# Plain fp32 products for the first mixing and for four of twelve convolution shifts, without a stagger

## The reference

```
def mixing(x, e, W0, b0, W1, b1, W2, b2, weight, bias_k):   # layers 0 and 2
    h = gelu(gelu(e @ W0 + b0) @ W1 + b1)
    att = softmax(h @ W2 + b2)                    # 8 experts
    agg_w = einsum('bk,koi->boi', att, weight)    # a 128x128 matrix for each sample
    return einsum('boi,bih->boh', agg_w, x) + (att @ bias_k)[:, :, None]

def conv(x, c, weight, c_weight, bias):           # layers 1 and 3: 9 taps, 4 groups of 32 channels
    out = conv1d(x, weight, padding=4, groups=4)
    return out + (c @ c_weight.T)[:, :, None] + bias[None, :, None]

x = x + mixing0(x); x = x + conv1(x); x = x + mixing2(x); x = x + conv3(x)
```

## Time and profile before

| | us |
|---|---|
| median of 3 runs | 2906.19 (2905.75 to 2907.77) |
| profiled execution, its own time | 2907.99 |
| its span | 2905.7 |
| TensorE busy | 2882.7 |
| VectorE busy | 2420.1 |
| ScalarE busy | 1668.6 |
| GpSimd busy | 1482.6 |
| DMA queue 1, share of 16 engines | 63.8% |

### The profile page before, as it was taken

The page is one execution under the profiler, slowest core; times in us unless marked ns, Lnnn a source line. Parts: engine busy times, 40 slices in busy tenths (PEclk is TensorE's granted clock), DMA queues, the critical chain, the costliest instruction groups (busy, mean ns, idle before and its releaser), DMA issues.

```text
span 2905.7 us, 122950 instructions
## 1 busy us (share of the span) xinstructions
PE 2882.7 (99%) x49240; PEld 2860.9 (98%) x49240; DVE 2420.1 (83%) x2589; ACT 1668.6 (57%) x2593; POOL 1482.6 (51%) x1546
## 2 busy tenths in 40 slices
PE   8999999999999999999999999999999999999998
PEld 7999999999999999999999999999999999999998
DVE  8888888888888888888888888888888888888884
ACT  5555555555555555556565656565556555655564
POOL 3445554555455545544554455445544554455452
PEclk9999999999999999999999999999999999999999
DMA  6777777777777777777777777777777777777774
GB/s 160 198 199 201 202 196 203 198 202 196 202 197 202 198 202 196 204 196 204 193 204 197 204 193 206 198 203 194 204 199 203 197 200 200 202 203 193 201 202 138
DMA packets 374536, 573.17 MB, mean 197 GB/s; under 512 B 63336, under 2 KB 226800, under 8 KB 358128
## 3 DMA queue, kind: packets, MB, share of 16 engines
q1 hardware_dynamic: 325744, 506.17, 63.8%
q10 hardware_dynamic: 48768, 66.65, 9.1%
HBM read 271.63 MB, written 167.77 MB: 151 GB/s over the span
## 4 chain that ended last, share of the span: by engine, by line
PE 98%; DVE 1%; ACT 0%; DMA 0%; issue 0%; ACTq 0%; SPq 0%
PE ps L354 74%; PE ps L339 24%; ACT x_t L530 0%; DVE prod L592 0%; DVE y L635 0%; DVE m_sum L595 0%; PE ps L267 0%; PE ps L262 0%; DMA mixed<-m_own 0%; DVE m_own L603 0%; DMA m_parts<-mixed 0%; DVE m_own L601 0%; DVE xp L627 0%; DVE conv_parts L567 0%; ACT L449 0%
## 5 line engine op out<-in xcount | busy, mean ns | idle before, releaser
L354 PE MATMUL ps<-y,conv_parts 32*128 32x512 f32 x36864 | 2735.2, 390 | 2.2 <-DVE y L635 2.2
L354 PEld LDWEIGHTS ps<-y,conv_parts 32*128 32x128 f32 x36864 | 2533.4, 184 | 17.5 <-issue 2.3
L500 ACT ACTIVATE y<-ps,bias 128x512 fp32r<-128x512 f32 x1536 | 1045.4, 690 | 748.6 <-PE ps L354 710.6
L635 DVE SCALAR_TENSOR_TENSOR y<-ps,bias,y 128x512 fp32r<-128x512 f32 x1536 | 1074.4, 747 | 417.4 <-ACT y L500 415.0
L703 POOL COPY bias<-bias_table 128x4 f32 (+3 forms) x512 | 99.1, 209 | 1383.3 <-DMA o_ch<-o_ph 1344.5
L709 POOL TENSOR_TENSOR xp<-x_t,xp 128x512 fp32r<-128x512 f32 x508 | 787.4, 1581 | 3.9 <-ACT xp L469 3.9
L339 PE MATMUL ps<-xp,m_parts 32*128 32x512 f32 x6144 | 653.2, 391 | 7.5 <-DVE y L635 3.7
L339 PE MATMUL ps<-y,m_parts 32*128 32x512 f32 x6144 | 652.4, 390 | 0.0
L716 POOL COPY o_t<-o_ch 128x512 f32<-128x512 f32 x508 | 630.1, 1358 | 8.4 <-DMA o_ch<-o_ph 8.4
L533 ACT ACTIVATE o_ph<-ps,bias 128x512 f32<-128x512 f32 x508 | 330.5, 686 | 435.6 <-PE ps L354 431.1
L339 PEld LDWEIGHTS ps<-xp,m_parts 32*128 32x128 f32 x6144 | 557.9, 184 | 10.3 <-issue 4.1
(11 more groups left out here) (53 smaller groups left out, 53.3 us busy)
## 6 DMA issues: line engine op xcount, KB each, us to landing
x_t<-x SPq DMA_DIRECT2D x512, 256.0 KB, 5.6
m_parts<-mixed SPq DMA_DIRECT2D x1020, 128.0 KB, 3.7
out<-o_t SPq DMA_DIRECT2D x127, 1024.0 KB, 4.0
o_ch<-o_ph SPq DMA_DIRECT2D x1016, 64.0 KB, 2.0
o_ch<-o_ph ACTq DMA_DIRECT2D x1016, 64.0 KB, 3.7
mixed<-m_own SPq DMA_DIRECT2D x256, 128.0 KB, 2.1
conv_raw<-conv_w SPq DMA_DIRECT2D x2, 768.0 KB, 11.8
mix_sb<-mix_w SPq DMA_DIRECT2D x2, 576.0 KB, 9.1
```

Source lines behind the costliest of these rows:

```text
L354: ins = nc.tensor.matmul(ps[:, 4 + t, :], conv_parts[layer][rows, w, PH * q + p_in, :], src[rows, a, p_in, q:q + N], start=(k == 0), stop= ...
L500: nc.scalar.activation(dst, src, ACT.Identity, bias=bias[layer][:, k % WIDTH[layer]:k % WIDTH[layer] + 1]).then_inc(high_set[layer], 1)
L635: nc.vector.scalar_tensor_tensor(out=dst, in0=src, scalar=bias[layer][:, k % WIDTH[layer]:k % WIDTH[layer] + 1], in1=high.bitcast(fp32), o ...
```

## The change

- **First mixing** works on whole x in plain fp32: four products of 128 rows by 128 columns by 512, with m_sum[0] as it comes from VectorE. x is no longer split, m_parts, the store and the load remain for the second mixing alone, and the spreading product for sample 0 is gone. x comes by one DMA in its own order.
- **Convolutions.** The shifts 2 to 9 (DENSE) stay in three f32r passes on four row tiles, 24 rounds. The shifts 0, 1, 10 and 11 have no weights for some output phases; they (SPARSE) are made in plain fp32 on tiles of 32 rows by 64 columns, 16 products a convolution in two sets of eight that lie on eight different tiles. They read a plain fp32 copy (y1_full, y3_full) that ScalarE makes with an additional evacuation of layers 0 and 2, and the unrounded conv_raw. Convolution 3 begins with them, convolution 1 ends with them.
- **LOW** of layers 0 and 2 is made from that copy in SBUF, so those banks are free when ScalarE is done (high_set).
- **No stagger**: the four tiles of a stage start and end together.
- **ScalarE issues no DMAs**; SyncE issues all of them, in a new order.
- **The tail**: the last sample's o_ph is regrouped by 16 small fp32 products (last_regroup) and copied to x_t in time order by ScalarE and VectorE, a quarter at a time.

```diff
+    DENSE = range(2, SHIFTS - 2)
+    SPARSE = (((1, 0, 2), (10, 2, 2)),
+              ((0, 0, 2), (11, 2, 2)))
 # SyncE
+                if has(i, inner, 0) and has(i, inner, -1):
+                    sp.wait_ge(mm[0], 4 * (i + 1))
+                    load_x(i + 1)
                 if has(i, inner, 3):
                     sp.wait_ge(in_time_set, 4 * (i - 2))
                     sp.dma_start(out[i - 3], o_t[:]).then_inc(out_done, 16)
+                if moves:
+                    for g in range(G // 2):
+                        shuffle(i - 2, g)
+                if has(i, inner, 0):
+                    store_matrix(i)
+                if moves:
+                    for g in range(G // 2, G):
+                        shuffle(i - 2, g)
+                if has(i, inner, 0):
+                    load_matrix(i, not inner and i == 0)
 # TensorE
+            def first_mix(i, inner):
+                pe.wait_ge(summed[0], i + 1)
+                pe.wait_ge(x_in, 16 * (i + 1))
...
+                for q in range(G):
+                    if inner or i >= 2:
+                        pe.wait_ge(high_set[2], nth(i - 2, q))
+                    nc.tensor.matmul(ps[:, q, :], m_sum[0][:], x_t[:, q, :], start=True, stop=True).then_inc(mm[0], 1)
+            def sparse(layer, src, begins, wait_bank):
+                for r, units in enumerate(SPARSE):
+                    for t in range(G):
+                        rows = slice(CG * t, CG * (t + 1))
+                        if r == 0 and begins:
+                            wait_bank(t)
+                        for s, p, width in units:
+                            q, p_in = divmod(s, PH)
+                            final = r == len(SPARSE) - 1 and not begins
+                            ins = nc.tensor.matmul(ps[CG * p:CG * (p + width), 4 + t, :],
+                                                   conv_raw[layer][rows, 128 * s + CG * p:128 * s + CG * (p + width)],
+                                                   src[rows, p_in, q:q + N], start=(r == 0 and begins), stop=final)
+                            if final:
+                                ins.then_inc(mm[1], 1)
+            def step(i, inner):
...
+                if now:
+                    first_mix(i, inner)
+                if not inner and i == 0:
+                    att_to_all(1)
+                if before:
+                    if not inner and i == 2:
+                        pe.wait_ge(conv_set, 2)
+                    pe.wait_ge(high_set[2], 4 * (i - 1))
+                    sparse(3, y3_full, True, free3)
+                    pe.wait_ge(low_set[2], 4 * (i - 1))
+                    dense(3, y3, False, free3)
+                if last:
+                    second_mix(i, inner)
+                if now:
+                    if not inner and i == 0:
+                        pe.wait_ge(zeros_set, 1)
+                        pe.wait_ge(conv_set, 1)
+                    pe.wait_ge(low_set[0], 4 * (i + 1))
+                    dense(1, y1, True, free1)
+                    if not inner and i == 0:
+                        side_bias()
+                        pe.wait_ge(full_first, G)
+                    sparse(1, y1_full, False, free1)
+            def last_regroup():
+                pe.wait_ge(phases_set, 4 * B)
+                for p in range(PH):
+                    for g in range(G):
+                        rows = slice(CG * p, CG * (p + 1))
+                        nc.tensor.matmul(ps[CG * g:CG * (g + 1), p, :], consts_sb[rows, CG * p:CG * (p + 1)], o_ph[rows, g, :],
+                                         start=True, stop=True).then_inc(regroup_mm, 1)
 # ScalarE
+            def high(layer, j, k, src, dst, full=None):
...
+                if full is not None:
+                    nc.scalar.activation(full, src, ACT.Identity, bias=column)
+                nc.scalar.activation(dst, src, ACT.Identity, bias=column).then_inc(high_set[layer], 1)
 # VectorE
+            def low(layer, j, k, dst, full, high):
+                dve.wait_ge(high_set[layer], nth(j, k))
+                nc.vector.tensor_tensor(dst, full, high.bitcast(fp32), ALU.subtract).then_inc(low_set[layer], 1)
             def step(i, inner):
...
+                elif now:
+                    if inner or i + 1 < B:
+                        matrix(0, i + 1)
+                    for q in range(G):
+                        low(0, i, q, segment(y1[:, LOW], q), segment(y1_full, q), segment(y1[:, HIGH], q))
+                    matrix(2, i)
+                    halves(i)
```

More of the change, by code:

```diff
@@ L128, in build_cond_resid @@
         x_in = sem("x_in")
[L129 removed]
+        m_in = sem("m_in")
         shuffled = [sem(f"shuffled{p}") for p in range(PH)]
@@ new lines, in dense @@
+            def dense(layer, src, begins, wait_bank):
+                order = sorted(DENSE, key=lambda s: (s % PH, s))
+                for k, s in enumerate(order):
+                    q, p_in = divmod(s, PH)
+                    for n, (w, a) in enumerate(PASSES):
+                        first = k == 0 and n == 0 and begins
+                        final = k == len(order) - 1 and n == len(PASSES) - 1 and not begins
+                        for t in range(G):
+                            rows = slice(CG * t, CG * (t + 1))
+                            if first:
+                                wait_bank(t)
+                            ins = nc.tensor.matmul(ps[:, 4 + t, :], conv_parts[layer][rows, w, s - DENSE[0], :],
+                                                   src[rows, a, p_in, q:q + N], start=first, stop=final)
+                            if final:
+                                ins.then_inc(mm[3], 1)
@@ L535, in step @@
-                if not inner and i == 0:
-                    conv_high_part(3)
+                        nc.scalar.activation(o_ph[:, g, :], ps[:, 4 + g, :], ACT.Identity,
+                                             bias=bias[3][:, g:g + 1]).then_inc(phases_set, 1)
+                    if final:
+                        act.wait_ge(regroup_mm, G * PH)
+                        act.wait_ge(mm[0], 4 * B)
+                        for q in range(G):
+                            dst, src = last_in_time(q, 0)
+                            nc.scalar.copy(dst, src).then_inc(last_set[q], 1)
@@ new lines, in step @@
+                    att_rows(5, 1, 1)
+                    matrix(2, 0, first=True)
+                    halves(0, first=True)
+                    dve.wait_ge(table_act, 2)
+                    dve.wait_ge(table_dve, 2)
+                    matrix(0, 1)
+                elif now:
+                    if inner or i + 1 < B:
+                        matrix(0, i + 1)
+                    for q in range(G):
+                        low(0, i, q, segment(y1[:, LOW], q), segment(y1_full, q), segment(y1[:, HIGH], q))
+                    matrix(2, i)
+                    halves(i)
@@ L681, in _ @@
             for beside in (y1, y3):
-                last = nc.gpsimd.memset(beside[:, :, :, 0:HALO:HALO - 1].bitcast(fp32), 0.0)
+                nc.gpsimd.memset(beside[:, :, :, 0:HALO:HALO - 1].bitcast(fp32), 0.0)
+            for beside in (y1_full, y3_full):
+                last = nc.gpsimd.memset(beside[:, :, 0:HALO:HALO - 1], 0.0)
             last.then_inc(zeros_set, 1)
```

398 lines of the change are left out of this document (130 added, 268 removed).

## The result

| | before | after |
|---|---|---|
| median, us | 2905.97 (4 runs) | 2831.89 (4 runs, 2830.63 to 2833.21) |
| span of the profiled execution | 2905.7 | 2830.7 |
| period of a sample in the steady part | 22.31 | 21.76 |
| all that is not 126 periods | 94.6 | 88.9 |

The ratio is 0.9744, 95% interval 0.9727 to 0.9761. The forecast was 2849 us with a period of 21.92 and 86.8 us for the rest.

What follows compares the result with a forecast made beforehand. TensorE was taken as the bound. Start and end of 86.8 us plus 126 x 21.92 gave a span of 2848.7 us; adding 2.3 and subtracting 1.8 gave 2849 us, range 2775 to 2965.

Steps and rivals of the forecast that it cites:

- The bound: Whole kernel: TensorE busy 2882.7 of 2905.7 us at granted clock 1.0 throughout, with a period of 22.31 us a sample.
- An fp32 record: TensorE, plain fp32: each product shows as two records, each 0.436 us for 512 columns, bounds 0.427 and 0.465.
- Eight tiles at once: Sparse phases: eight 64-column tiles run together, 1.74 us instead of 2.79, gaining 1.05 twice a sample.
- The rival of the column halves: Sparse phases: column halves of one row group take turns, 3.49 us instead of 1.74; 3296 us, chance 0.07.
- The second record: Sparse phases: a product's second record holds up the next tile, 7.41 us a phase; 4301 us, chance 0.08.
- Shape changes: TensorE: four changes of tile shape a sample, 0.70 us together, bounds 0 and 1.2.
- The faster rival: TensorE: shape changes hidden, 0.427 us a record, but the first stall grows to 0.36; 2776 us, chance 0.14.
- The first stall: First mixing to convolution 3: TensorE waits for banks to be emptied, 0.1 us a sample, bounds 0 and 0.4.
- The second stall: Second mixing to convolution 1: TensorE waits for ScalarE to free four banks, 0.2 us a sample, bounds 0 and 0.5.
- The sum: Per sample on TensorE: records 6.98, 60 rounds 13.94, shape changes 0.70, stalls 0.30, together 21.92 us against 22.31.
- The engines beside: Other engines: VectorE about 80% busy, ScalarE 75%, GpSimd near 27%; matrix and x loads priced at nothing.
- Start and end: Outside the 126 steady periods: 86.8 us instead of 94.6; step 1 begins at 31.0, step 2 at 49.3, end 37.5.

Runs made afterwards that it cites:

- e1: Kernel after with the fp32 shifts on 128-column tiles, four products at a time instead of eight: 3225.83 us, ratio 1.1100 to the kernel before.
- e2: Kernel after with the same 16 sparse products a phase queued tile by tile: 2866.44 us, ratio 0.9860 to the kernel before.
- e4: Kernel after with each convolution's f32r shifts and sparse rounds alternated in halves, adding four tile shape changes a sample: 2934.5 us, ratio 1.0099 to before.
- e5: Kernel after with first mixing as 12 f32r rounds on constant tiles, layer 0 not computed: 2829.14 us, ratio 0.9735 to the kernel before.
- e6: Kernel after with VectorE writing the fourth bank of o_ph, ScalarE the first three: 2818.27 us, ratio 0.9697 to the kernel before.
- e7: Kernel after with six shifts in fp32, adding two rounds of sixteen 32 by 32 tiles: 2837.38 us, ratio 0.9765 to the kernel before.
- e9: e7 with one more round of sixteen zero-weight 32 by 32 tiles in each convolution: 3107.99 us, ratio 1.0694 to the kernel before.
- e3: Kernel after with all twelve shifts back in three f32r passes: 3076.11 us, ratio 1.0582 to the kernel before.
- e8: Kernel after with the changes of e6 and e7 together: 2819.76 us, ratio 0.9706 to the kernel before.

## Why the prediction was right, point by point

**The bound.** As said, TensorE before and after, and the period carries the result: 126 x (22.31 - 21.76) = 69 us of the 75 by which the span fell. One reading was too smooth: the earlier trace rows show 90% or more in every slice, not 1.0 throughout. In the trace of before the granted clock is 0.5 from 36.1 to 39.5 us and from 56.6 to 60.0, and so the 94.6 us outside the steady part already held time at half clock.

**An fp32 record.** Put at 0.436 us within 0.427 and 0.465; the eight records of first mixing lie 0.429 us apart (the first gap, which holds part of the shape change, is 0.53), the low end, as the small fp32 products of the earlier trace rows had it. Sixteen of them are 0.11 us less than forecast.

**Eight tiles at once.** The step that decided the sign. It held: in the window from 1508.1 to 1508.25 of the kernel after, the first records of eight products are already at work,

```profile
1508.18 0.69 PE L343 MATMUL ps<-y_full,conv_raw 32*64 32x512 f32 x8
```

0.69 us for all eight where one alone is modelled at some 0.6, and e1 shows the price without it. The rival of the column halves would have given 3296 us; e1, which is that rival made by hand but has two shape changes fewer, gave 3226.

**The second record.** The rival by which one product's second record holds up the next tile is refuted, by the kernel after and more strongly by e2. So the rule of the Trainium skill, page TensorE: Matmul & The Clock Gate, section Part 3, that products start and end in strict order, does not hold for plain fp32 products on different tiles; the measurement decides. Giving it 0.08 was fair from a trace that had no such case, and what spoke against it was the right sign.

**Shape changes.** Put at 0.70 for four. In the stage table they are inside the intervals: 3.63 for first mixing is 8 x 0.429 = 3.43 and 0.20; 1.90 for a sparse phase is 4 x 0.429 = 1.72 and 0.18. The sum of four is 0.7 to 0.8, and e4 puts 0.20 on each. That the shape costs it and not the format is shown with e4, by e1. The faster rival, changes hidden behind the queue, is out.

**The first stall** (convolution 1 to first mixing to convolution 3) was put at 0.1. It is 0: convolution 3's sparse part starts 3.63 after first mixing, with no gap beyond the shape change. The term was mis-sized by 0.1, because the 0.2 us for registers in the loop does not come here: L477 starts 0.11 after L314 does, an estimated 0.19 after the end of the last sparse product's stream (its start at 1509.57 and 0.427), where 0.2 to 0.4 had been allowed. And TensorE goes on 0.07 after VectorE's last low half (1510.91 + 2.73 = 1513.64) where 0.1 to 0.26 had been allowed. What the prediction did not see is how close this balance is: e5 shows that here evacuation and first mixing are the same 3.6 us.

```profile
1510.19 2.42 ACT L477 ACTIVATE y<-ps,bias 128x512 fp32r<-128x512 f32 x4 [2.89 <-PE ps L343]
1510.91 2.73 DVE L609 SCALAR_TENSOR_TENSOR y<-ps,bias,y 128x512 fp32r<-128x512 f32 x4 [2.89 <-ACT y L477]
```

**The second stall** (o_ph) was put at 0.2; e6 takes away 0.15. Its place and its releaser were right.

**The sum.** 16 records 6.86, 60 rounds 13.94 to 14.0, changes 0.7 to 0.8, second stall 0.15: 21.7 to 21.8, measured 21.76. The forecast's 0.16 too much are the records (0.11) and the first stall (0.1), less some hundredths in the f32r rounds.

**The engines beside.** VectorE was put at 80% and is at 69%. The subtractions took 0.81 rather than 0.69 us, but the multiplication (L592 before, L573 after) fell from 2.09 to 1.64 and the two halves (L601 and L603, now L585 and L587) from 1.02 and 0.85 to 0.23 and 0.29:

```profile
L573 DVE TENSOR_TENSOR prod<-mix_sb,att_table 128x1152 f32<-128x1152 f32 x254 | 416.6, 1640 | 0.0
...
L587 DVE TENSOR_TENSOR m_own<-m_sum,m_own 128x128 fp32r<-128x128 f32 x128 | 37.4, 292 | 4.4
L585 DVE CAST m_own<-m_sum 128x128 fp32r<-128x128 f32 x128 | 29.1, 227 | 15.8
```

I had carried over means of operations that are long when GpSimd is at work beside them, although showed it. In the trace of before, the 27 of 256 L603 that no GpSimd instruction overlaps take 0.29 us each and the others 0.91 on average; in the kernel after none is overlapped, and all 128 take 0.29. No run varied GpSimd's work alone. GpSimd itself came to 31% for 27. ScalarE came to 65% for 75, as its evacuations overlap in part (0.577 apart at 0.7 each). In the steady part neither is on the path; ScalarE's 1% of the chain comes from the start and the end, where TensorE waited for it (7.8 us in all). The matrix and x came in time; no wait on a DMA is in the chain.

**Start and end.** Put at 86.8, measured 88.9. The end came to 36.9 against 37.5: the 5.4 us stall is there as 4.9, the regrouping took 1.15 for 1.5, the copies 2.0 to 2.5 for 3.8. But the stall brought what the prediction left out: TensorE stood still for 4.86 us and then ran at half clock for the sparse phase, 3.52 us from start to start instead of 1.90. The last line is from the view by stretches: stretch, length, TensorE busy and records, granted clock, DMA share, GB/s.

```profile
2812.67 3.59 PE L343 MATMUL ps<-y_full,conv_raw 32*64 32x512 f32 x32 [4.86 <-ACT y L477]
2816.19 5.86 PE L361 MATMUL ps<-y,conv_parts 32*128 32x512 f32 x96
...
2823.71 1.15 PE L415 MATMUL ps<-o_ph,consts_sb 32*32 32x512 f32 x32 [1.67 <-DVE o_ph L648]
...
2812.70:2816.00 3.30, 3.30 (x32) 0.50 0.40 98
```

The start is where the 2.1 us went: step 1 begins at 32.54, not 31.0, and step 2 at 52.04, not 49.3, 2.7 late against the 0.6 that the end gave back. Second mixing in step 1 waits one bank at a time as foreseen. In this execution the small products of line 261 ran at half clock:

```profile
11.20 3.21 PE L261 MATMUL ps<-consts_sb,att_sb 128*128 128x128 f32 x16
14.34 0.71 PE L291 MATMUL ps<-att_t,mix_b_sb 8*128 8x128 f32 x4
```

3.21 us where the earlier trace rows has 2.05, and first mixing begins at 15.63 instead of 13.5.

The rest of the delay is in step 1. Its second mixing waits bank by bank, the last time until 40.01, and then the granted clock is 0.50 from 41.0 to 44.4 us:

```profile
40.01 4.30 PE L329 MATMUL ps<-y,m_parts 32*128 32x512 f32 x44 [0.66 <-ACT y L477]
```

Convolution 1 starts 4.09 us after this start. In the trace of e4, where the clock stays at 1.0 here, it is 2.68 (38.24 to 40.92), so some 1.4 us are lost. The prediction's sum for start and end has no term for the clock. The three stretches at half clock in which TensorE had work, at 11, 41 and 2813 us, cost some 4.6 us, an estimate from the same work at full clock: 1.6 (the products of L285 and L261 take 4.09 us from start to start, in before 2.51), 1.4 and 1.6. That 86.8 came within 2.1 of 88.9 is in part luck, as shorter work in the tail made up for them.

## What to carry to other kernels

A product of three f32r passes is not always cheaper than one of plain fp32: where zero weights leave whole column groups unused, fp32 on half-width tiles makes the same product in 1.72 us for four shifts against 2.79, if the tiles really overlap. So cut the operands by their zeros first, and see in a trace that the tiles overlap: eight did fully, sixteen did not (e7). Each change of tile shape cost 0.2 us here. Where the tiles of a stage all end together, the wait before the banks' next use is bounded by how fast they are emptied. So group the shapes, and give the last bank of a hand-over to the engine that is idle. A dearer stage that just covers such a hand-over costs nothing, which is seen only when the stage is made shorter.

## What the runs showed of the hardware that was not expected

- Each of the column-tiled products takes its turn in the start at 7 ns when eight are issued, 13 ns when the queue goes tile by tile, and 17 ns in the second of two rounds of sixteen; such a round cost 1.06 us where its stream is 0.86 (e9).
- Records that wait for their tile do not hold up the products of other tiles behind them, at least three deep (e2).
- The granted clock of TensorE went to 0.5 (1.2 GHz) from about 10.2 to 13.7 us in the profiled execution of the kernel after, behind a pause of about 1 us. It came back to 1.0 before first mixing. With the same pause and the same work it fell so in the executions of e2, e3, e5, e8 and e9 too, and not in those of before, e1, e4, e6 and e7. From the view by stretches of the kernel after (stretch, length, TensorE busy and records, granted clock, DMA share, GB/s):

```profile
10.00:11.00 1.00, 1.00 (x6) 0.62 0.97 399
11.00:12.00 1.00, 1.00 (x5) 0.50 1.07 437
12.00:13.00 1.00, 1.00 (x6) 0.50 1.00 411
13.00:14.00 1.00, 1.00 (x8) 0.67 1.09 455
```

What made the difference between executions stays open; nothing here varied it.
